# A graph layer and a mixture of experts on one core: TensorE's signals counted per pair of segments

## What is computed

```python
x = x + gnn(layernorm(x))          # gnn(x) = x @ W1.T + b1 + mean @ W2.T + b2
# mean[n] = sum of x[dst of e] over the edges e with src == n, over their count
x = x + moe(layernorm(x))          # 8 experts of 256 -> 1024 -> 256, the best 2 of each node
```

## Time and profile before

| | us |
|---|---|
| median of 3 runs | 2147.4 |
| the profiled execution | 2149.78 |
| its span in the trace | 2148.0 |
| start to the first segment | 129 |
| gather stage, 129 to 1344 | 1215 |
| experts, 1344 to the end | 804 |
| TensorE busy in all | 1819.4 |
| GpSimd busy in all | 1221.2 |

### The profile page before, as it was taken

How to read it: one execution, slowest core, us unless ns; L and a number is a source line. 1 busy time by engine, 2 the same in 40 slices (tenths; PEclk the granted TensorE clock), 3 DMA queues, 4 the chain that set the end, 5 groups by cost and what they waited for, 6 DMA issues and landing times.

```text
span 2148.0 us, 40435 instructions
## 1 busy us (share of the span) xinstructions
PE 1819.4 (85%) x10822; PEld 1522.5 (71%) x10822; DVE 1016.7 (47%) x2245; ACT 893.4 (42%) x2581; POOL 1221.2 (57%) x1146
## 2 busy tenths in 40 slices
PE   6967887778877687877776777899999999999998
PEld 4745664567745565655555566899999999999997
DVE  6858875877757676743444447641111111111111
ACT  5721661147511154621112158654444444444443
POOL 2046666677766677776666663345444554444443
PEclk9979998989988899989999889999999999999999
DMA  6222222323332332333333355772444242442421
GB/s 179 70 86 81 84 82 85 87 84 87 87 87 85 89 88 86 87 91 90 90 86 89 91 169 186 252 238 35 119 118 110 45 116 39 115 115 40 115 38 17
DMA packets 104623, 211.55 MB, mean 98 GB/s; under 512 B 26710, under 2 KB 69884, under 8 KB 98614
## 3 DMA queue, kind: packets, MB, share of 16 engines
q0 software_dynamic: 61376, 129.59, 24.4%
q1 hardware_dynamic: 29664, 67.66, 9.4%
q10 hardware_dynamic: 13462, 12.84, 1.8%
HBM read 361.34 MB, written 35.04 MB: 185 GB/s over the span
## 4 chain that ended last, share of the span: by engine, by line
PE 69%; DVE 10%; issue 8%; another core or an unknown queue 6%; ACT 4%; DMA 2%; DVEq 1%; POOL 0%; ACTq 0%; SPq 0%; POOLq 0%
PE bank L1163 20%; PE bank L1196 17%; PE bank L1212 17%; PE bank L945 5%; DVE agg L1816 3%; PE bank L1041 2%; PE bank L999 2%; ACT arena L686 1%; PE bank L1184 1%; DVE arena L1521 1%; DVE arena L1287 1%; ACT arena L706 1%; DVE arena L1318 1%; DVE arena L1349 1%
## 5 line engine op out<-in xcount | busy, mean ns | idle before, releaser
L568 POOL DMA_INDIRECT arena<-ytab,arena x784 | 824.0, 1051 | 375.1 <-issue 205.5
L1163 PE MATMUL bank<-arena 128*128 x2356 | 660.6, 419 | 81.5 <-DVE agg L1816 30.6
L1163 PEld LDWEIGHTS bank<-arena 128*128 128x128 f32 x2356 | 464.4, 209 | 178.3 <-issue 114.3
L838 ACT ACTIVATE arena<-bank,agg 128x128 f32<-128x128 f32 x848 | 311.1, 368 | 410.0 <-PE bank L1196 337.8
L1816 DVE TENSOR_TENSOR agg<-agg,bank 128x257 f32 x589 | 247.2, 420 | 408.0 <-PE bank L1163 235.8
L1196 PEld LDWEIGHTS bank<-arena,agg 128*128 128x128 f32 x3392 | 396.8, 193 | 5.5 <-ACT arena L838 0.2
L1196 PE MATMUL bank<-arena,agg 128*128 128x128 f32 x3392 | 398.6, 276 | 0.0
L706 ACT ACTIVATE arena<-arena 128x1024 f32<-128x1024 f16 x148 | 156.4, 1056 | 581.3 <-DVE arena L1521 408.8
L1212 PE MATMUL bank<-agg,arena 128*128 128x256 f32 x1696 | 384.2, 379 | 1.0 <-DMA agg<-in_b 0.9
L601 POOL DMA_INDIRECT out<-arena x106 | 172.5, 1627 | 326.4 <-issue 241.4
L1212 PEld LDWEIGHTS bank<-agg,arena 128*128 128x128 f32 x1696 | 313.8, 190 | 40.3 <-DMA agg<-in_b 1.4
(11 more groups left out here) (265 smaller groups left out, 1450.0 us busy)
## 6 DMA issues: line engine op xcount, KB each, us to landing
agg<-in_w SPq DMA_DIRECT2D x212, 1024.0 KB
agg<-in_b SPq DMA_DIRECT2D x106, 128.0 KB
arena<-ytab,arena POOLq DMA_INDIRECT x784
ytab<-arena SPq DMA_DIRECT2D x12, 512.0 KB, 2.9
node<-in_x SPq DMA_DIRECT2D x6, 896.0 KB, 12.3
out<-node ACTq DMA_DIRECT2D x6, 896.0 KB
xtab<-xn ACTq DMA_DIRECT2D x35, 128.0 KB
xtab_a<-xn ACTq DMA_DIRECT2D x14, 128.0 KB
```

The costliest lines, as they stand in the source:

```text
L568: pool.indirect_dma_start(out=rows[:, v % RU, h, 0:D], out_offset=None, in_=ytab[:, :], in_offset=bass.IndirectOffsetOnAxis(ap=rowidx[g % ...
L838: act.activation(hT[:, m, :], hidden_bank(j, m)[:, 0:T], ACT.Relu, bias=b1b[:, b, m:m + 1]).then_inc(s_fr, 1)
L1163: mm = pe.matmul(bank[bank_of(n)][:, 0:W], onehot[n // QUAD % 2][:, n % QUAD, h, :], pair[:, h * W:(h + 1) * W], start=(h == 0), stop=(h = ...
```

## The change

TensorE signals at the end of every second segment of a group, and at the end of the group's last (the last group's 173 are odd). That leaves 56 + 68 + 84 + 87 = 295 of 589 signals. All that wait for `s_agg` round their count of segments up to pairs: `pairs_to(n)`, (n + 1) // 2. For ScalarE's waits, which are for multiples of 4, that is the same moment as before. The table `until` is made with one more added, and an integer shift halves it: one new vector instruction in each of the four groups.

```diff
+def pairs_to(n):
+    return (n + 1) // 2
...
-                sp.wait_ge(s_agg, done[k % 16] if k < UNITS[g] - 1 else SEG0[g] + RUN[g])
+                sp.wait_ge(s_agg, done[k % 16] if k < UNITS[g] - 1 else pairs_to(SEG0[g] + RUN[g]))
...
-                    act.wait_ge(s_agg, QUAD * (q - 1))
+                    act.wait_ge(s_agg, pairs_to(QUAD * (q - 1)))
...
-                    mm.then_inc(s_agg, 1)
+                    if k % 2 == 1 or k == RUN[g] - 1:
+                        mm.then_inc(s_agg, 1)
...
-                begun(v.scalar_tensor_tensor(out=until[b][0:1, 0:UNITS[s]], in0=misc[0:1, SMAX:SMAX + UNITS[s]], scalar=float(SEG0[s]),
+                begun(v.scalar_tensor_tensor(out=until[b][0:1, 0:UNITS[s]], in0=misc[0:1, SMAX:SMAX + UNITS[s]], scalar=float(SEG0[s] + 1),
                                              in1=iota_c[0:1, 0:UNITS[s]], op0=ALU.add, op1=ALU.add))
                 step(v.tensor_tensor(unit[:, 0:n], iota_c[:, 1:n + 1], misc[:, 0:n], ALU.subtract))
                 v.sem_inc(s_unit)
+                begun(v.tensor_scalar(until[b][0:1, 0:UNITS[s]], until[b][0:1, 0:UNITS[s]], 1, None, ALU.logical_shift_right))
...
-                    v.wait_ge(s_agg, n + 1)
+                    v.wait_ge(s_agg, pairs_to(n + 1))
```

More of the change, by code:

```diff
@@ L362, in gnn_moe @@
         s_row = [sem(f"rows_in{r}") for r in range(RU)]
-        s_units, s_free, s_oh16, s_oh, s_agg, s_sum = (sem(n) for n in ("units_in", "units_free", "onehot16_ready", "onehot_ready", "segment_multiplied", "segment_summed"))
+        s_units, s_free, s_oh16, s_oh, s_agg, s_sum = (sem(n) for n in ("units_in", "units_free", "onehot16_ready", "onehot_ready", "segments_multiplied", "segment_summed"))
         s_w1s, s_w1c, s_tr1, s_xT1, s_mm1, s_add1, s_bias = (sem(n) for n in (
```

## The result

The changed kernel takes 2188.0 us, the median of 4 runs between 2185.4 and 2189.8. The kernel before, timed beside it on the same chip, takes 2145.1 us (median of 4 runs, 2136.1 to 2148.5). The ratio is 1.0212, 95% interval [1.0191, 1.0232]: slower by 43 us, where I had named "no change" as the likeliest case, 2150 us with a range of its own of 2128 to 2171. The measured time lies inside the wider range that I gave for 8 times in 10, 2092 to 2206, but only because that range took in the slower rival. In the ratios of all experiments one execution is left out: one of the ten of experiment 12 took 2887.1 us, at a granted clock of 0.567 where the others have 0.951 to 0.959. The lines of the changed kernel are numbered 6 to 8 higher: the segment's matmuls are L1169, the sum L1824, the fetch L574, the wait for a free slot L457.

A forecast was written before the change was run, and what follows sets the result against it. The prediction took GpSimd's fetches, held up 166.4 us waiting for freed slots, to bound the gather stage. It summed 2149.8 - 46 + 45 + 3 + 1 = 2152.8, as run median 2150 us; own range 2128 to 2171, wider 2092 to 2206.

The forecast's parts named there:

- no change: Whole kernel: saving and cost nearly cancel, 2150 us, own range 2128 to 2171; chance 0.42.
- the slower rival: Gather stage: halving signals saves nothing while pairs wait for their second segment; 2196 to 2226 us, chance 0.30.
- What bounds the kernel: Gather stage, 1215 us: GpSimd's fetches feed it; its 166.4 us of waits for freed slots are the most to gain.
- Fewer signals: TensorE in the gather stage: 28% fewer signals, each with its own chance of being held, save 46 us of GpSimd's waits.
- The first of a pair is told later: Vector engine's sums: 50 waits 1.5 us later add 75 us of TensorE idle time, 0.60 passed on, +45 us.
- the faster rival: Gather stage: fewer signals make holds much rarer and avoid falls of the clock; 2095 us, chance 0.28.
- Slots freed later: SyncE's wait for a unit ends up to one segment later, against a reserve of 4 units: +3 us.
- the new instruction: Vector engine in the gather stage: four times near 0.19 us, at most 0.8 us in all, entered as +1.
- The last 51 segments: End of the gather stage, 3 banks: TensorE has one segment left to run on in, counted inside the +45.
- ScalarE's widening: ScalarE's waits are for multiples of four segments: same moment as before, 0.
- The signs that I had given for it: Gather stage: waits of 3 us and more on "remote" stay as many; TensorE's listed waits grow with GpSimd's.
- The signs for my own forecast: Gather stage: slot wait 166 +- 25 us, waits before sums below 352 us, TensorE's listed waits from 200 to about 275.

The follow-up runs named there:

- experiment 12: Changed kernel with TensorE's share of the work beside the segments done three segments later instead of two (LAG 3), third chip: 2034.0 us, ratio 1.0054.
- number 1: Kernel before with all 589 signals, but the vector engine and SyncE wait for whole pairs of segments: 2188.1 us, ratio 1.0205.
- experiment 2: Kernel before with all signals, only the vector engine waiting for whole pairs of segments: 2189.0 us, ratio 1.0212.
- experiment 3: Kernel before with 589 more signals, one on each segment's first matmul, that nobody waits for: 2144.6 us, ratio 1.0011.
- experiment 5: Kernel before with only SyncE's freeing of slots by pairs and the new vector instruction, second chip: 2023.1 us against 2024.4, ratio 0.999.
- experiment 11: Kernel before with the vector engine waiting for whole pairs except in the last 51 segments, third chip: 2055.2 us, ratio 1.0148.
- 7 and 8: Kernel before, second chip: 7 replaces indirect fetches by plain DMAs of 128 consecutive rows, 1896.5 us; 8 fetches 64 of 256 numbers per row, 2023.7 us.
- experiment 4: Changed kernel with TensorE's share of the work beside the segments done three segments later instead of two (LAG 3), first chip: 2153.0 us, ratio 1.0039.
- experiment 9: Changed kernel, unaltered, against the kernel before on the second chip: 2070.8 us against 2024.6, ratio 1.0229.
- experiments 6 and 10: Kernel before with TensorE's share of the work beside the segments three segments later (LAG 3), run twice: 2020.6 and 2020.1 us, ratios 0.9979 and 0.9975.

## Where the prediction was right and where wrong, step by step

**The number.** 2188.0 us lies 38 us above the forecast of 2150 and outside its own range of 2128 to 2171. It lies inside 2092 to 2206 because that range was stretched over the slower rival, which had 0.30: the range was right, the case that I held for likeliest was not.

**What bounds the kernel.** The reading of the stages held: start and experts within 2 us, all of the 40 us in the gather stage. GpSimd's wait for slots was the right measure, since it rose by 50.6 us where the time rose by 43.

**Fewer signals, -46 us: this is the step that failed.** I took each signal to have its own chance of being held, and multiplied 28% fewer signals with 166.4 us. Measured, the saving is nil, within some 10 us: all 589 signals sent and waited for late (experiments 1 and 2) give 1.0205 and 1.0212, the change 1.0212; 589 more of them (experiment 3) give 1.0011. The end of the range that I had written as "nothing, if a hold is a stretch of time that catches whatever comes" is what happened. The step had a second, smaller fault, which the other chips show: it took the wait for slots of the earlier trace rows to be made of holds from end to end. On a chip without holds 20.4 us of it are left (experiment 5), so about 146 us are put down to the holds, by comparing two chips; but nothing that the change does touched them.

**The first of a pair is told later, +45 us: right in size, partly by luck.** By itself (experiment 2) it costs 2189.0 - 2143.4 = 45.6 us, with an interval of some 11 us either way. I had reckoned 75 us more of waiting on TensorE, of which 0.60 would pass to the end. The waits of the earlier trace rows grew by 40.6 us instead, to 240.7 and not 275, in 146 waits and not 100, and even that counts some pauses twice, as my 200.1 did, since PE and PEld rows overlap. TensorE's idle time as a whole grew by 21 us in the gather stage. The other 19 us of its 40 are the same instructions at a lower granted clock, in the last 51 segments, a term that my sum did not have: I had falls of the clock in the faster rival only, as something saved. So the path of the idle time is the one I named, but it carries about half of the loss, and that the product of two wrong factors gave the whole is luck. Nor was the lengthening spread over the rows: 26.3 of the 40.6 us stand at L1357.

**Slots freed later, +3, and the new instruction, +1: measured 0** (experiment 5, 0.999 [0.9969, 1.0012], and number 1 against number 2). The units' reserve of four may be what hid it; that was not tried. The new instruction took 0.18 to 0.21 us, four times, as the earlier trace rows had it.

**The last 51 segments** were put "inside the +45". They are, but they carry about a third of it (experiment 11; nearly half by the trace of the first chip) with 51 of 589 segments, which the prediction did not say: lateness is some five times as dear for each segment there, an estimate from that third. And it is no longer idle time but a granted clock of 0.73 instead of 0.86.

**ScalarE's widening, 0:** nothing in the runs speaks against it, since the vector engine's waits alone give the whole loss.

**The sum with the measured terms:** 2145.1 + 0 + 45.6 + 0 + 0 = 2190.7, against 2188.0 measured. The 45.6 contain the slower clock.

**The rivals.** The slower one, "the late first segment decides", is the one that came true, with its place (L1824, and L1047, L926, L951 and L1068 waiting behind it) and its condition, that fewer signals save nothing. Its price of 2196 to 2226 us began 8 us too high, 4 of them for slots and the instruction that cost nothing. The signs that I had given for it are both there: held signals as many as before (38 and 33), and the earlier trace rows up together with GpSimd's waits. The signs for my own forecast failed: the wait for slots was to stay within 166 +- 25 and is 217, the waits before the sums were to fall below 352 us, in about half as many, and are 384.2 us in 165 of 188, and the earlier trace rows was to reach about 275 and is at 240.7. The faster rival is out: fewer signals did not give fewer holds.

**What stays open** is what holds the signals on the first chip. The two kernels that were to tell (7 and 8) ran where nothing is held. That the fetches set them off was only argued. And what lowers the granted clock in the last 51 segments is open too.

## What to carry to other kernels

Counting completions in groups saves the sender nothing that shows here, and makes the first of each group late by the time of the others behind it. Price that by what is queued behind the waiting instruction on its engine and by who needs that at a fixed distance: the vector engine, idle for 465 of the stage's 1215 us, was still on the path, since its work comes two segments ahead of its use. If the grouping must stay, lengthen that distance (LAG 3 took back three quarters), and leave the places with fewer buffers ungrouped. Here nothing spoke for it to stay.

When a wait in a profile has several parts, ask of each which edit would reach it before you take a share of the whole. And compare with the kernel before on the same chip: two chips here differ by 119 of 2143 us on one program, more than twice what the change does.

## What the runs showed of the hardware

The same program takes 2143.4 us on one chip and 2024.4 us on two others, 119 us or 5.6% apart. On the first, 110 to 182 us of the vector engine's waits before the sums end in "remote", with signals up to some 8 us late; on the other two no profile has such a wait there. GpSimd's wait for slots is 166.4 us with held signals and 20.4 us without (experiment 5), and its idle "issue" steps are 21 us longer there, 226.5 instead of 205.5: 125 us less idle, which covers the difference of 119. That the holds are the whole of what sets the chips apart is argued from this, not shown. Yet the change costs the same on both, 1.0212 and 1.0229, so the holds don't make the loss. Nor do they follow the number of signals: with half of the segments' signals 160.1 and 181.8 us (the changed kernel, experiment 4), with all of them 116.8, 132.9 and 109.8 (before, experiments 1 and 2), with twice as many 139.0 (experiment 3), from one profile each.

At LAG 2, TensorE's granted clock is lower in the last 51 segments when the vector engine waits for pairs there. On the first chip it is 0.86 before and 0.83 with twice the signals, but 0.73 in the changed kernel and in experiments 1 and 2. On the second chip it is 0.84 in experiment 5 and 0.76 in experiment 9, and 0.82 in experiment 11 on the third, which has single waits there. With LAG 3 the changed kernel has 0.78 there on the first chip (experiment 4), but 0.89 on the third (experiment 12), as the kernel before with LAG 3 (0.88 and 0.89, experiments 6 and 10). These are the rows of experiments 5 and 9:

```profile
1105.00:1221.00 116.00, 95.79 (x529) 79.71 (x530) 72.50 (x299) 78.70 (x247) 69.59 (x71) 0.84 0.63 198
```

```profile
1140.00:1269.00 129.00, 106.59 (x529) 88.05 (x529) 69.81 (x291) 76.93 (x242) 66.00 (x69) 0.76 0.56 175
```

The same 529 records are busy for 10.8 us more, at 0.76 instead of 0.84, and the stretch is 13 us longer. TensorE's idle time in the stretch is nearly the same, 20.2 and 22.4 us. So nearly all of what the stretch loses appears as TensorE being slower, not idle; before it, on this chip as on the first, the loss is for the greater part idle time. Why the clock is lower, no run here shows.
